# The tensor engine reads a tile's span numbers in two halves, the second one between its second and third couple

## The reference

```
def _rgcn_conv(x, W, Wroot, b, src, dst, etype):
    xs = x[src]
    seg = dst * R + etype
    sums = jax.ops.segment_sum(xs, seg, num_segments=N * R)
    cnt = jax.ops.segment_sum(jnp.ones_like(xs[:, 0]), seg, num_segments=N * R)
    mean = sums / jnp.maximum(cnt, 1.0)[:, None]
    mean = mean.reshape(N, R, -1)
    return x @ Wroot + b + jnp.einsum('nrd,rde->ne', mean, W)

h = _rgcn_conv(layernorm(x), W1, Wroot1, b1, src, dst, edge_type)
h = _rgcn_conv(relu(h), W2, Wroot2, b2, src, dst, edge_type)
x = x + h
x = x + experts(layernorm(x))     # gate, top 2 of 8, gelu(x @ W1[e] + b1[e]) @ W2[e] + b2[e]
```

## Time and profile before

| | us |
|---|---|
| median of 3 runs | 3608.35 (3605.62 to 3616.27) |
| the profiled execution's own time | 3620.74 |
| its span, from the first to the last instruction | 3618.8 |
| PE busy | 2451.1 (68%) |
| DVE busy | 1783.5 (49%) |
| POOL busy | 1842.2 (51%) |
| mean granted clock of TensorE | 0.828 of full speed |

### The profile page before, as it was taken

How to read it: one execution, slowest core, us unless ns; L and a number is a source line. 1 busy time by engine, 2 the same in 40 slices (tenths; PEclk the granted TensorE clock), 3 DMA queues, 4 the chain that set the end, 5 groups by cost and what they waited for, 6 DMA issues and landing times.

```text
span 3618.8 us, 82716 instructions
## 1 busy us (share of the span) xinstructions
PE 2451.1 (68%) x19188; PEld 1806.6 (50%) x19189; DVE 1783.5 (49%) x4914; ACT 1206.2 (33%) x2300; POOL 1842.2 (51%) x1908
## 2 busy tenths in 40 slices
PE   1344566667778885445567777788886028899998
PEld 0112344445566674113344555666776027788886
DVE  6322333444556663222333444455555437777776
ACT  4000122233345552011122233445552115545544
POOL 1665555655555553665556665555530643333333
PEclk9555678898999997555778899899995569999999
DMA  6233323333333332223233333333332323222221
GB/s 208 86 99 90 113 88 93 96 95 97 100 103 102 104 105 68 84 80 89 85 93 92 98 99 97 98 102 105 104 102 80 138 86 126 79 67 69 67 66 55
DMA packets 178124, 344.66 MB, mean 95 GB/s; under 512 B 36174, under 2 KB 115498, under 8 KB 177928
## 3 DMA queue, kind: packets, MB, share of 16 engines
q0 software_dynamic: 90864, 245.38, 23.0%
q10 hardware_dynamic: 49488, 59.36, 5.1%
q1 hardware_dynamic: 37704, 39.16, 3.6%
HBM read 283.55 MB, written 62.39 MB: 96 GB/s over the span
## 4 chain that ended last, share of the span: by engine, by line
PE 41%; issue 25%; DVE 12%; another core or an unknown queue 7%; DVEq 6%; ACT 5%; DMA 2%; POOL 2%; ACTq 1%; SPq 0%; POOLq 0%
PE bank L1214 13%; PE sum_banks L1194 8%; PE sum_banks L1195 6%; PE sum_banks L1334 4%; PE bank L1334 3%; PE bank L1206 3%; DVEq L872 3%; DVEq L869 2%; DVE sel_more L872 2%; POOL lot_in L454 1%; DVE sel L864 1%; ACT stage L542 1%; ACT edge_work L648 1%; PE sum_banks L1297 1%
## 5 line engine op out<-in xcount | busy, mean ns | idle before, releaser
L435 POOL DMA_INDIRECT ring<-table,row_tab x1568 | 1508.9, 962 | 1116.7 <-SPq L357 726.6
L1214 PE MATMUL bank<-weights,stage 128*128 128x256 f16 x5292 | 884.8, 292 | 37.6 <-ACT stage L542 24.5
L1194 PE MATMUL sum_banks<-ring,sel_more 128*128 x780 | 254.6, 327 | 554.6 <-issue 406.0
L1214 PEld LDWEIGHTS bank<-weights,stage 128*128 128x128 f16 x5292 | 519.6, 104 | 186.0 <-issue 75.7
L1194 PE MATMUL sum_banks<-ring,sel 128*128 x1568 | 462.9, 296 | 215.1 <-issue 119.6
L576 ACT ACTIVATE stage<-sum_banks,inv 128x256 f16<-128x256 f32 x784 | 328.0, 472 | 824.6 <-issue 286.0
L864 DVE SCALAR_TENSOR_TENSOR sel<-lane,win_off,key_tab 128x256 f16<-128x256 f16 x792 | 349.3, 482 | 479.6 <-PE bank L1214 274.9
L542 ACT ACTIVATE stage<-bank 128x1024 f16<-128x1024 f16 x392 | 401.9, 1025 | 324.0 <-remote 246.6
L872 DVE TENSOR_SCALAR sel_more<-lane,win_off,key_tab 128x128 f16 x780 | 262.3, 336 | 473.5 <-issue 306.5
L1195 PE MATMUL sum_banks<-ring,sel 128*128 x1568 | 463.3, 296 | 6.5 <-issue 5.9
L1194 PEld LDWEIGHTS sum_banks<-ring,sel_more 128*128 x780 | 79.9, 102 | 743.6 <-issue 738.9
(11 more groups left out here) (270 smaller groups left out, 2784.9 us busy)
## 6 DMA issues: line engine op xcount, KB each, us to landing
ring<-table,row_tab POOLq DMA_INDIRECT x1568
weights<-L_ffn_W ACTq DMA_DIRECT2D x96, 178.5 KB
stage<-L_ffn_W ACTq DMA_DIRECT2D x16, 1024.0 KB
edge_work<-lot_in SPq DMA_DIRECT2D x55, 260.0 KB
lot_in<-zero ACTq DMA_DIRECT2D x47, 260.0 KB
table<-edge_work SPq DMA_DIRECT2D x7, 896.0 KB, 4.5
table<-edge_work ACTq DMA_DIRECT2D x49, 128.0 KB
out<-acc SPq DMA_DIRECT2D x6, 1024.0 KB
```

The lines of the kernel that those rows point to most:

```text
L435: pool.indirect_dma_start(ring_rows[:, b % RING, 0:2 * D], None, tables[layer], bass.IndirectOffsetOnAxis(row_tab[:, b:b + 1], 0)).then_in ...
L1194: pe.matmul(to[:, 0:D + 1], hot, flat(slot[:, :, D:2 * D + 1]), start=first, stop=last, skip_group_check=True)
L1214: return [pe.matmul(ps_out[par], rows[:, xp * KD + k, :], w16[:, wp, k, r * D:(r + 1) * D], start=part == 0 and n == 0, stop=part == PARTS ...
```

## The change

`load_meta` reads ten integers in place of 20: four windows and the one behind them. `tile_work` calls it twice: before couple k = 0 as until now, and again between couples k = 1 and k = 2. The registers of a half are given back after its two couples. `couple` numbers its windows within the half (j = 0 to 3). The matmuls, their operands and their order are the same, and so is every wait. The diff is whole but for unchanged lines:

```
             def load_meta(w):
                 loads[0] += 1
-                regs = [... for k in range(2 * WPT + 4)]
-                pe.load(regs, meta_row[0:1, ds(2 * w, 2 * WPT + 4)])
-                lo = [... for k in range(WPT)]
-                return regs, lo, [... for k in range(WPT + 1)]
+                regs = [... for k in range(WPT + 2)]
+                pe.load(regs, meta_row[0:1, ds(2 * w, WPT + 2)])
+                lo = [... for k in range(WPT // 2)]
+                return regs, lo, [... for k in range(WPT // 2 + 1)]
...
-                        j = 2 * k + h
+                        j = 2 * (k % 2) + h
...
                 def tile_work(t, par, age):
-                    regs, lo, mark = load_meta(t * WPT)
-                    for k in range(STEPS):
-                        couple(t, par, age, k, lo, mark)
+                    for half in range(2):
+                        regs, lo, mark = load_meta(t * WPT + half * (WPT // 2))
+                        for k in (2 * half, 2 * half + 1):
+                            couple(t, par, age, k, lo, mark)
+                        for r in regs:
+                            pe.free_register(r)
                     if layer == 0 and age == 1:
                         weights_turn(1)
-                    for r in regs:
-                        pe.free_register(r)
```

## The result

The changed kernel is slower: 3641.32 us, median of 5 runs (3638.42 to 3647.59), against 3614.6 of the kernel before (five runs). The ratio is 1.0066 [1.0047, 1.0085], so +24 us [+17, +31]. The forecast was 3595 us, which is 13 us less than the 3608 it started from, and a range up to 3614; it named the wrong side. Two further comparisons of the same two kernels gave 1.0078 and 1.0077.

A forecast was written before the change was run, and what follows sets the result against it. PE, the busiest engine, was taken to bound the kernel through its sequencer's register loads. Of 60 us saved 40 were kept, of 31 + 4 added 27; 27 - 40 = -13 us, 3608 - 13 = 3595 us, range 3579 to 3614.

The forecast's parts named there:

- What bounds the kernel: Whole kernel: PE is busiest at 68%; time its sequencer gives back or takes should mostly be seen in the whole.
- The price of a load of ten: PE's register load: 0.72 us from a line through loads of four, eight and 20; bounds 0.62 and 0.90.
- The sign the prediction set for itself: Tile's start and couple 2: wrong if the first gap doesn't shrink by 0.6 us or the second is over 0.8.
- The first half: Load before couple 0: 0.64 us shorter, first sum earlier by that or the gap; 60 us saved over 98 tiles.
- The second half: Load before couple 2: 1.63 us needed, 1.08 covered at full clock; 0.55 us late at 57 places, 31 us.
- The lead: Behind the second load the sequencer is barely ahead of PE; branch gaps cost 4 us, bounds 0 and 23.
- rival B: Couples 2 and 3: lost sequencer lead empties PE's queue at branches, 0.35 to 0.5 us each; 3619 us, chance 0.12.
- What passes through: Whole kernel: 40 of 60 us saved at tile starts reach the end, and 27 of 35 us added.
- C: Both PE loads: a load has a large fixed part, ten take 0.90 us; slower, 3624 us, chance 0.03.
- A: Tile's start: saving swallowed by DVE's load of 20 and ACT's means; within 0.3%, 3605 us, chance 0.30.
- D: Whole kernel: all 60 us pass and the clock stays up in the layers' middle; 3573 us, chance 0.06.
- The rule weighed there: PE's loads: floor of about 600 ns makes ten cost 0.98 us, saves only 0.38 a tile, splitting pays twice; slower.

The follow-up runs named there:

- second10: Changed kernel with the first PE load of a tile back at 20 numbers, the second load of ten kept; 1.0265 of the kernel before, +84 us.
- split12: Changed kernel with 12 numbers in each half's PE load in place of ten, the last two unused; 1.0043 of the kernel before, +15 us.
- one18: Kernel before with one PE load of 18 numbers a tile in place of 20; 1.0033 of the kernel before, +12 us.
- one24: Kernel before with one PE load of 24 numbers a tile in place of 20, four unused; 1.0036 of the kernel before, +13 us.
- pe12_4_4: Kernel before with PE's load of 20 cut into 12 at the tile's start, four before couple 2, four before couple 3; 1.0018 of the kernel before.
- split10_dve: Changed kernel with DVE's load of 20 also cut, 12 at the tile's start and eight before couple 2; 1.0081 of the kernel before.
- pe16_4: Kernel before with PE's load of 20 cut into 16 at the tile's start and four before couple 3; 0.9993 of the kernel before.
- dve12_8: Kernel before with DVE's load of 20 cut into 12 at the tile's start and eight before couple 2, PE's load unchanged; 0.9994 of the kernel before.

## Why the prediction was wrong

**What bounds the kernel: right.** PE's sequencer time is seen in the whole: second10 adds 98 loads with their address operations and nothing else, and pays 84 us.

**The price of a load of ten: wrong, and the step that failed.** "Ten come to 0.335 + 6 x 0.064 = 0.72 us", with 0.62 and 0.90 as bounds. It is 1.077, outside both. The line went through 4, 8 and 20, all multiples of four, and ten isn't one; the bound from a single number took the 0.488 us on L1141 as fixed part and spread the rest evenly, which again assumed that each number costs the same. The sign the prediction set for itself came out so: the first gap shrank by 0.32 us (median 1.19 to 0.87) where 0.6 was asked. Put into the forecast's own sums, the measured price gives the result:

- The start saves 98 x (1.362 - 1.077) = 28 us, not 63; by the forecast's share of 40 in 60 that is 19.
- The second load needs 0.14 + 1.08 + 0.27 + 0.47 + 0.03 = 1.99 us, less 1.08 of cover 0.91, not 0.55. At 57 places that is 52, with the 4 of the lead 56, by the forecast's share of 27 in 35 that is 43.
- 43 - 19 = +24 us. Measured: +24 [+17, +31].

The agreement to the microsecond is luck, since the shares were estimates, and the same sums miss split12 (0 for +15). From the runs: about half of a change at the start passes (one18, one24), so 14; couple 2 is 0.85 us longer in the late tiles, and 48 of these make 41; 41 - 14 = +27, with a share that is known only roughly.

**The first half: mechanism right, size wrong.** The load to the first sum is 1.56 us, the load plus 0.48 of register work, as the step said.

**The second half: mechanism right.** The cover of 1.08 us, the free load at the lower clock and the cost at full clock came as stated; 0.82 us in the rows and 0.85 in the means stand against 0.91 by the sum.

**The lead: about right here.** After the second load of ten the loops over further blocks showed no new cost: couple 3 takes 3.49 us in both. The prediction's rival B isn't what made it slower. But pe12_4_4 points to a spent lead being paid at the next load.

**What passes through: too hopeful at the start.** Two thirds were taken. One18 and one24 give about half with wide intervals, but in the splits less passes: of 0.36 us in the first layer couple 1 takes back 0.32, and of the 0.72 of split12 0.55. This term is the second one that failed: in split12, where the price of 0.85 us lies inside the forecast's bounds, the sums say 0 us and the run +15. The reasons given are only partly borne out: cutting DVE's load (7 us) brought no gain (split10_dve), the wait for ACT grew by 3 to 7 us, where 8 us were set aside for it, and the clock wasn't in the sum.

**The rivals.** C was the right one, with a chance of 0.03: "a load has a large fixed part", 3624 us by 0.90 us. Its price was right in direction; its reason isn't, for there is hardly a fixed part (0.08 us), the dear part is the two numbers left over. Its 3624 us also leaves out the share of 27 in 35 that the forecast took off; with it C would have said 3613. The chance was too low because "the line through 4, 8 and 20" counted as three witnesses when they were one. A had half of the start's saving right (it is swallowed), but the load of DVE isn't shown to be the reason, and it had the end wrong. D is out: the clock didn't stay up, and in the late tiles of the first layer it fell from 0.99 to 0.97.

**The rule weighed there.** The Trainium skill (DMA: Bandwidth & Descriptors, "Latency and other measured facts") gives a `tensor_load` a floor of about 600 ns. The runs don't agree: one number takes 0.304 to 0.308 us and four 0.33 to 0.35. What the prediction drew from that floor, that splitting pays it twice, pointed to the right side for a reason that these loads don't show.

## What to carry to other kernels

A line through prices holds only for sizes of the same kind: look at what the known sizes have in common (here multiples of four) before a size between them is read off. Load registers in fours that start at a multiple of four; rounding a count up can make the load shorter. A stop of the sequencer that is moved into a covered place can cost twice, for what sticks out there and for the lead that the next stop lacks. Compare the cover with the stop and its register work, at the clock of those tiles, before you count it as free; even then little came back here (pe16_4: 0.9993 of before). What a shorter start gives can be taken back by the next wait, so a term for it needs an experiment of its own.

## What the runs showed of the hardware beyond that

- The price list of a register load from fast memory on PE: 0.08 us, 0.257 for an aligned four, 0.238 for each other number; a start at element 1 or 2 makes all of them single, a start at 8 doesn't (12 from element 2: 2.875 us against 0.853 from element 0; ten from element 8: 1.073).
- The compiler drops register loads whose numbers nothing reads; a load that is to be timed needs a reader.
- The same kernel took 3162 us in one session and 3558 to 3620 us in the others. That this is a difference between chips isn't shown: the record gives the chip the same number, 8, in the session with 3162 us and in one with 3620 us. POOL's gather instructions for the ring took the same time each (963 and 962 ns), but ACT stood idle before its copies on L542 for 15.5 us in the first (dve12_8) and 324.0 us in another (before):

```profile
L542 ACT ACTIVATE stage<-bank 128x1024 f16<-128x1024 f16 x392 | 403.1, 1028 | 15.5 <-PE bank L1209 15.4
```

```profile
L542 ACT ACTIVATE stage<-bank 128x1024 f16<-128x1024 f16 x392 | 401.9, 1025 | 324.0 <-remote 246.6 <-PE bank L1206 71.8 <-issue 4.2
```

What ACT waits for there is mostly called "remote" and isn't resolved by the profile. In tiles 20 to 43 of the first layer couple 1 takes 3.84 us in the first and 4.7 in the other, so in the late tiles the gap lies mostly in the couple that took back the start's saving. But tiles 24 to 47 of both layers make only 46 of the 458 us between these two profiles; most of it lies in the dense tiles at the start of each layer. Second10 was run only in the session with 3162 us, so its 84 us doesn't carry over as a sum, only what it adds to couple 2.
